# One indirect transfer of 128 rows per expert pair, replaced by two of 64 rows, in a decoder layer with 64 experts

## The reference

```python
x = _layernorm(x + attention(x))
x = _layernorm(x + cross_attention(x, ctx))
x = _layernorm(x + _moe(x))                      # E = 64, K = 8, H = 256, I = 96, CAP = 64

def _moe(hidden_states, gate_w, wg, wu, wd):
    x = hidden_states.reshape(-1, Hd)            # T = 1024 tokens
    probs = jax.nn.softmax(x @ gate_w.T, axis=-1)
    w, sel = jax.lax.top_k(probs, K)
    w = w / jnp.sum(w, axis=-1, keepdims=True)
    eid, tok = sel.reshape(-1), jnp.repeat(jnp.arange(T), K)
    ...
    valid = pos < CAP                            # an expert takes its first 64 tokens
    xin = jnp.zeros((E, CAP + 1, Hd), x.dtype).at[eid, slot].set(x[tok])
    h = silu(einsum("ech,ehi->eci", inp, wg)) * einsum("ech,ehi->eci", inp, wu)
    out = einsum("eci,eih->ech", h, wd)
    y = jnp.zeros((T, Hd), x.dtype).at[tok].add(out_pad[eid, slot] * w * valid)
```

## Time and profile before

| | |
|---|---|
| median of 3 runs | 375.88 us (374.93 to 377.12) |
| the profiled execution | 371.15 us, of which the span from first to last instruction is 369.2 us |
| mean granted TensorE clock | 0.845 of full speed |
| PE busy | 266.0 us (72% of the span) |
| DVE busy | 232.5 us (63%) |
| POOL busy | 164.0 us (44%), of it 49.7 us in the 32 scatters of L599 |
| ACT busy | 131.8 us (36%) |
| DMA | 66.61 MB, mean 180 GB/s |

### The profile page before, as it was taken

The page is one execution under the profiler, slowest core; times in us unless marked ns, Lnnn a source line. Parts: engine busy times, 40 slices in busy tenths (PEclk is TensorE's granted clock), DMA queues, the critical chain, the costliest instruction groups (busy, mean ns, idle before and its releaser), DMA issues.

```text
span 369.2 us, 5446 instructions
## 1 busy us (share of the span) xinstructions
PE 266.0 (72%) x1793; PEld 167.1 (45%) x1793; DVE 232.5 (63%) x532; ACT 131.8 (36%) x234; POOL 164.0 (44%) x167
## 2 busy tenths in 40 slices
PE   8676696899889897898888787105899999980000
PEld 4462464567466574575455554002344554540000
DVE  0927754499876999678944777503335777750692
ACT  4510375017941169511494134000123444440021
POOL 2002022400253446825545077876144588874272
PEclk9695899899999999999989699655557999995555
DMA  7799908789999221961110299971999898655981
GB/s 251 226 123 276 311 10 119 110 241 301 385 323 194 80 93 71 164 125 71 66 63 3 65 333 317 288 219 34 267 285 304 211 159 144 75 64 101 364 324 57
DMA packets 47261, 66.61 MB, mean 180 GB/s; under 512 B 5979, under 2 KB 33241, under 8 KB 47234
## 3 DMA queue, kind: packets, MB, share of 16 engines
q1 hardware_dynamic: 39120, 56.52, 55.4%
q0 software_dynamic: 7680, 9.47, 13.7%
q10 hardware_dynamic: 434, 0.27, 0.2%
HBM read 36.45 MB, written 28.75 MB: 177 GB/s over the span
## 4 chain that ended last, share of the span: by engine, by line
PE 38%; DVE 27%; issue 9%; DMA 9%; ACT 8%; SPq 4%; POOL 3%; POOLq 0%; DVEq 0%; ACTq 0%
PE M L1314 14%; PE SA L1314 6%; DVE nmax L908 6%; PE O L1314 5%; PE SB L1314 5%; DMA early<-early 4%; SPq L379 4%; PE O L1787 3%; POOL xin_d L517 3%; ACT probs L640 2%; DVE early L1274 2%; DVE early L1280 2%; DVE xmax L899 1%; PE SB L1807 1%; DMA early<-acc_d 1%
## 5 line engine op out<-in xcount | busy, mean ns | idle before, releaser
L599 POOL DMA_INDIRECT acc_d<-xp_t,idx_out x32 | 49.7, 1552 | 30.1 <-ACT xp_t L821 19.1
L504 POOL DMA_INDIRECT xin_d<-row,idx_slot x48 | 47.7, 994 | 34.1 <-DVE nmax L908 12.0
L1314 PE MATMUL M<-middle 128*128 128x256 f32 (+3 forms) x144 | 29.0, 385 | 3.9 <-ACT middle L676 1.2
L1314 PE MATMUL SA<-early 96*128 96x256 bf16 (+1 forms) x128 | 22.4, 305 | 8.5 <-DMA early<-early 3.5
L808 ACT ACTIVATE xp<-M 128x96 f32<-128x96 f32 x32 | 8.0, 250 | 56.1 <-PE M L1314 56.1
L558 POOL TENSOR_TENSOR early<-early 128x1024 f32<-128x1024 f32 x3 | 6.4, 2140 | 46.5 <-ACT early L650 46.4
L1314 PEld LDWEIGHTS M<-middle 128*128 128x128 f32 (+1 forms) x144 | 20.6, 197 | 11.8 <-issue 6.2
L908 DVE TENSOR_REDUCE nmax<-SA 128x4 f32<-128x1024 f32 x16 | 19.5, 1218 | 9.1 <-PE SA L1314 9.1
L1787 PE MATMUL O<-con,probs 128*128 128x128 f32 x40 | 10.3, 345 | 19.6 <-DMA probs<-xin_d 19.6
L1314 PE MATMUL SB<-early 96*128 96x256 bf16 (+1 forms) x128 | 21.5, 296 | 3.5 <-DVE nmax L908 2.4
L1314 PE MATMUL O<-middle,early 128*128 128x256 f32 (+1 forms) x96 | 20.9, 364 | 2.7 <-DVE middle L948 2.5
(11 more groups left out here) (261 smaller groups left out, 623.9 us busy)
## 6 DMA issues: line engine op xcount, KB each, us to landing
acc_d<-zeros SPq DMA_DIRECT2D x3, 2176.0 KB, 17.1
early<-early SPq DMA_DIRECT2D x48, 128.0 KB, 5.1
early<-acc_d SPq DMA_DIRECT2D x24, 256.0 KB, 5.8
xin_d<-zeros SPq DMA_DIRECT2D x1, 5136.0 KB, 20.1
early<-wgu SPq DMA_DIRECT2D x12, 384.0 KB, 13.3
middle<-wgu SPq DMA_DIRECT2D x12, 384.0 KB, 7.7
probs<-xin_d SPq DMA_DIRECT2D x20, 160.5 KB, 2.7
gu_sb<-wgu SPq DMA_DIRECT2D x8, 384.0 KB, 6.4
```

Of the source, the lines that this page charges most:

```text
L504: nc.gpsimd.indirect_dma_start(xin_d, bass.IndirectOffsetOnAxis(ap=idx[:, t, k:k + 1], axis=0), rows[:, t, :], None, bounds_check=SLOTS - ...
L599: nc.gpsimd.indirect_dma_start(acc_d[p % CHAINS], bass.IndirectOffsetOnAxis(ap=idx_out[:, p:p + 1], axis=0), yw[:, p % YRING, :], None, bo ...
L1314: return nc.tensor.matmul(o, l, r, start=start, stop=stop)
```

## The change

Each pair's rows leave in two transfers of 64 rows, one for each expert. There are four chains: pair p's expert e goes to chain 2 x (p mod 2) + e, so that a chain is used again two pairs later. Inside one transfer each token occurs once, so a chain needs one row per token: keys are no longer doubled, nothing is added for the second expert, and the index tile `idx_out` gets a column for each half, both on partitions 0 to 63 (DVE writes them with two instructions in place of one). A chain has 1152 rows in place of 2176. At the end SP reads two tiles of one chain with one load, 16 loads in all. It waits for chains 0 and 1 first and issues four loads from them, then waits for chains 2 and 3. DVE adds 2 x 256 columns to 2 x 256, and one more sum of 256 closes the tile.

```diff
-ROWS = NTOK + CAP
+ROWS = NTOK + P
-CHAINS = 3
+CHAINS = 4
...
-        idx_out = sb("idx_out", [P, PAIRS], I32)
+        idx_out = sb("idx_out", [P, 2, PAIRS], I32)
...
-        acc_d = [nc.dram_tensor(f"acc_d{c}", [2 * ROWS, D], F32, kind="Internal").ap() for c in range(CHAINS)]
+        acc_d = [nc.dram_tensor(f"acc_d{c}", [ROWS, D], F32, kind="Internal").ap() for c in range(CHAINS)]
...
-            for c in range(CHAINS):
-                sp.wait_ge(S["scat"][c], 16 * len(range(c, PAIRS, CHAINS)))
-            for t in range(TILES):
-                for c in range(CHAINS):
-                    sp.dma_start(fin[:, t, 2 * c:2 * c + 2, :],
-                                 acc_d[c].rearrange("(r h) d -> r h d", h=2)[t * P:(t + 1) * P]).then_inc(S["gu"][t], 16)
+            def load_sums(u, chains):
+                for c in chains:
+                    sp.dma_start(fin[:, 2 * u:2 * u + 2, c, :],
+                                 acc_d[c][2 * u * P:2 * (u + 1) * P].rearrange("(t p) d -> p t d", t=2)
+                                 ).then_inc(S["gu"][2 * u], 16)
+
+            for c in range(2):
+                sp.wait_ge(S["scat"][c], 16 * (PAIRS // 2))
+            for u in range(2):
+                load_sums(u, range(2))
+            for c in range(2, CHAINS):
+                sp.wait_ge(S["scat"][c], 16 * (PAIRS // 2))
+            for u in range(2):
+                load_sums(u, range(2, CHAINS))
+            for u in range(2, TILES // 2):
+                load_sums(u, range(CHAINS))
...
+                pool.wait_ge(S["idx_out"], 2 * (p + 1))
                 pool.wait_ge(S["yw"], p + 1)
-                if p >= CHAINS:
-
-                    pool.wait_ge(S["scat"][p % CHAINS], 16 * (p // CHAINS))
-                nc.gpsimd.indirect_dma_start(acc_d[p % CHAINS], bass.IndirectOffsetOnAxis(ap=idx_out[:, p:p + 1], axis=0),
-                                             yw[:, p % YRING, :], None, bounds_check=2 * ROWS - 1, oob_is_err=True,
-                                             compute_op=ALU.add).then_inc(S["scat"][p % CHAINS], 16)
+                for e in range(2):
+                    c = 2 * (p % 2) + e
+                    h = slice(e * CAP, (e + 1) * CAP)
+                    if p >= 2:
+
+                        pool.wait_ge(S["scat"][c], 16 * (p // 2))
+                    nc.gpsimd.indirect_dma_start(acc_d[c], bass.IndirectOffsetOnAxis(ap=idx_out[0:CAP, e, p:p + 1], axis=0),
+                                                 yw[h, p % YRING, :], None, bounds_check=ROWS - 1, oob_is_err=True,
+                                                 compute_op=ALU.add).then_inc(S["scat"][c], 16)
...
-                        act.wait_ge(S["scat"][(p - YRING) % CHAINS], 16 * ((p - YRING) // CHAINS + 1))
+                        for e in range(2):
+                            act.wait_ge(S["scat"][2 * ((p - YRING) % 2) + e], 16 * ((p - YRING) // 2 + 1))
...
-                    nc.vector.tensor_scalar(idx_out[:, p:p + 1], gath(p)[:, D + E:ROW], half, None, ALU.add
-                                            ).then_inc(S["idx_out"], 1)
+                    for e in range(2):
+                        nc.vector.tensor_scalar(idx_out[0:CAP, e, p:p + 1], gath(p)[e * CAP:(e + 1) * CAP, D + E:ROW], 0.0, None,
+                                                ALU.add).then_inc(S["idx_out"], 1)
...
-                dve.wait_ge(S["gu"][t], fin_base[t] + 16 * CHAINS)
-                nc.vector.tensor_tensor(fin[:, t, 0:3], fin[:, t, 0:3], fin[:, t, 3:6], ALU.add).then_inc(S["fpair"], 1)
-
-            def thirds_added(t, c):
+                u = t - t % 2
+                dve.wait_ge(S["gu"][u], fin_base[u] + 16 * CHAINS)
+                nc.vector.tensor_tensor(fin[:, t, 0:2], fin[:, t, 0:2], fin[:, t, 2:4], ALU.add).then_inc(S["fpair"], 1)
+
+            def quarters_added(t):
                 dve.wait_ge(S["fpair"], t + 1)
-                if c == 2:
-                    dve.wait_ge(S["fadd"], 2 * t + 1)
-                nc.vector.tensor_tensor(fin[:, t, 0], fin[:, t, 0], fin[:, t, c], ALU.add).then_inc(S["fadd"], 1)
+                nc.vector.tensor_tensor(fin[:, t, 0], fin[:, t, 0], fin[:, t, 1], ALU.add).then_inc(S["fadd"], 1)
...
-                    thirds_added(i, 1)
...
-                    thirds_added(i, 2)
+                    quarters_added(i)
...
-    con[:, CONST["key"]] = 2 * (np.arange(NT) * P + p)
-    con[:, CONST["dump"]] = 2 * (NTOK + p % CAP)
+    con[:, CONST["key"]] = np.arange(NT) * P + p
+    con[:, CONST["dump"]] = NTOK + p % CAP
```

More of the change, by code:

```diff
@@ L232, in loaded @@
             return S["gu"][n % RING], 32 * (n // RING + 1)
-        ACCS = 2 * CHAINS
+        ACCS = CHAINS
         fin = early[:, 0:TILES * ACCS * D].rearrange("p (t f d) -> p t f d", t=TILES, f=ACCS)
@@ L294, in build @@
             S[n] = ctx.enter_context(nc.semaphore(n))
-        S["gu"] = [ctx.enter_context(nc.semaphore(f"gu_in{r}")) for r in range(max(RING, TILES))]
+        S["gu"] = [ctx.enter_context(nc.semaphore(f"gu_in{r}")) for r in range(max(RING, TILES - 1))]
         S["gath"] = [ctx.enter_context(nc.semaphore(f"gathered{r}")) for r in range(GRING)]
@@ L369, in iteration @@
                         sp.dma_start(acc_d[n].rearrange("(p r) d -> p r d", p=P),
-                                     zeros[:, 0:D].unsqueeze(1).broadcast_to([P, 2 * ROWS // P, D])
+                                     zeros[:, 0:D].unsqueeze(1).broadcast_to([P, ROWS // P, D])
                                      ).then_inc(S["zero_out"], 16)
@@ L394, in rows_out @@
                 sp.wait_ge(S["zero_out"], 16 * (1 + CHAINS))
-                sp.dma_start(acc_d[0][0:2 * NTOK].rearrange("(b t p h) d -> b h p t d", t=NT, p=P, h=2)[b, 0],
+                sp.dma_start(acc_d[0][0:NTOK].rearrange("(b t p) d -> b p t d", t=NT, p=P)[b],
                              rows[:, :, 0:D]).then_inc(S["row_out"], 16)
@@ L430, in _ @@
                     sp.wait_ge(S["hid"], 2 * (p + 1))
-                    sp.wait_ge(S["idx_out"], p + 1)
+                    sp.wait_ge(S["idx_out"], 2 * (p + 1))
                     load_rows(p + GRING)
@@ L593, in scatter @@
             def scatter(p):
-                pool.wait_ge(S["idx_out"], p + 1)
+                pool.wait_ge(S["idx_out"], 2 * (p + 1))
                 pool.wait_ge(S["yw"], p + 1)
-                if p >= CHAINS:
-                    pool.wait_ge(S["scat"][p % CHAINS], 16 * (p // CHAINS))
-                nc.gpsimd.indirect_dma_start(acc_d[p % CHAINS], bass.IndirectOffsetOnAxis(ap=idx_out[:, p:p + 1], axis=0),
-                                             yw[:, p % YRING, :], None, bounds_check=2 * ROWS - 1, oob_is_err=True,
-                                             compute_op=ALU.add).then_inc(S["scat"][p % CHAINS], 16)
+                for e in range(2):
[6 more added lines that the diff above has]
+                                                 compute_op=ALU.add).then_inc(S["scat"][c], 16)
             for p in range(PAIRS):
@@ L1036, in route @@
                     need(dve, "keycol", b, 1)
-                    nc.vector.tensor_scalar(keycol[:], keycol[:], 2.0 * T, None, ALU.add).then_inc(S["keycol"], 1)
+                    nc.vector.tensor_scalar(keycol[:], keycol[:], float(T), None, ALU.add).then_inc(S["keycol"], 1)
                 def slots():
@@ L1243, in _ @@
             pipelined(iteration, last_batch)
-            half = con[:, CONST["half_of_row"]][:, 1:2]
             for i in range(PAIRS + 1):
@@ L1272, in halves_added @@
             def halves_added(t):
-                dve.wait_ge(S["gu"][t], fin_base[t] + 16 * CHAINS)
-                nc.vector.tensor_tensor(fin[:, t, 0:3], fin[:, t, 0:3], fin[:, t, 3:6], ALU.add).then_inc(S["fpair"], 1)
-            def thirds_added(t, c):
+                u = t - t % 2
+                dve.wait_ge(S["gu"][u], fin_base[u] + 16 * CHAINS)
+                nc.vector.tensor_tensor(fin[:, t, 0:2], fin[:, t, 0:2], fin[:, t, 2:4], ALU.add).then_inc(S["fpair"], 1)
+            def quarters_added(t):
                 dve.wait_ge(S["fpair"], t + 1)
-                if c == 2:
-                    dve.wait_ge(S["fadd"], 2 * t + 1)
-                nc.vector.tensor_tensor(fin[:, t, 0], fin[:, t, 0], fin[:, t, c], ALU.add).then_inc(S["fadd"], 1)
+                nc.vector.tensor_tensor(fin[:, t, 0], fin[:, t, 0], fin[:, t, 1], ALU.add).then_inc(S["fadd"], 1)
             def row_stats(t):
-                dve.wait_ge(S["fadd"], 2 * t + 2)
+                dve.wait_ge(S["fadd"], t + 1)
                 nc.vector.bn_stats(fstats[:, t], fin[:, t, 0]).then_inc(S["fstat"], 1)
```

## The result

The changed kernel takes 413.82 us (median of 4 runs, 411.76 to 417.42), the kernel before on the same chip 375.4 us (4 runs): 1.107 times as long, 95% interval 1.094 to 1.121. The forecast was 386.3 us, with a range up to 402. It was slower, as forecast, but by 38 us in place of 10.

What follows compares the result with a forecast made beforehand. POOL was taken to set when sums may be read and, with 2.54 us per pair against PE's 2.00, to become the bound: last landing +16.0, end -5.6, so +10.4 on 375.88 gives 386.3 us, range 374 to 402.

Steps and rivals of the forecast that it cites:

- X: POOL's price for one 64-row accumulating scatter, estimated at 0.97 us between bounds of 0.78 and 1.55.
- 54 X: POOL's issue of two 64-row scatters for each of 27 pairs, 5 to 31, in the total 54 X - 43.5 + w.
- The upper bound of 1.55: Ceiling set on X: a 64-row scatter costs at most a whole 128-row one, 1.55 us.
- rival 3: On POOL, a scatter's price doesn't fall at all with half the rows, X = 1.55: 417 us; chance 0.06.
- rivals 2 and 3: Scatter price on POOL: 2, plain price fixed, X = 1.26, 400.9 us, chance 0.22; 3, price unchanged, 417 us, 0.06.
- w: POOL's waits for earlier scatters of a chain to land, on top of issue: 1.5 us taken, 0 to 4.2 possible.
- rival 1: On POOL, scatter generation is all per row, X = 0.78, with w about 3: 377.3 us; chance 0.17.
- Pairs 0 to 4 in the slow part: Half-clock stretch, scatters 3.53 us apart: 2.54 us per pair on POOL fits, so pair 5 starts at 282.76 as before.
- The end: Loads and closing sums after the last landing: 1.3 us saved to the first sum, 4.3 over eight tiles, 5.6 together.
- Terms held at nothing: DVE's extra index instruction, ACT's wait for both halves, PE's pace or clock drop, smaller zeroing: nothing at the end.
- Rivals 1 and 4: Scatter price on POOL: 1, all per row, 377.3 us, chance 0.17; 4, accumulating surcharge a stall, 367 us, 0.10.
- The 43.5: Constant subtracted in the forecast difference from the kernel before, 54 X - 43.5 + w, in us.

Runs made afterwards that it cites:

- the price table: Kernel before plus 84 indirect transfers of 14 kinds after its last store; accumulating 64 rows took 1.42 us on POOL; its total time says nothing.

## Why the prediction was wrong

**The price of a 64-row scatter: the step that failed.** I took X = 0.97 us, on the assumption that 0.58 us of the plain price and all of the 0.58 us for accumulating are work per row. Measured: 1.40 us, of which 1.25 are there with no rows. Per row it is 2.4 ns, a quarter of what I had assumed (1.16 us for 128 rows is 9 ns per row). The term 54 X is 75.8 us in place of 52.4: +23.4. This alone puts the forecast at 409.7. Each of the two numbers that I had, 0.97 plain and 1.55 accumulating at the same 128 rows, says nothing on how a price depends on rows; I treated their difference as if it did. The upper bound of 1.55 was the nearer one, and what was said against rival 3 ("accumulating more rows must cost something") was right by 0.15 us only. The truth lay between rivals 2 and 3, to which I gave 0.28 together, with a range that ended below rival 3.

The Trainium skill's figure of about 1 us for the software path's emission (DMA: Bandwidth & Descriptors, "Latency and other measured facts") pointed the right way: plain transfers have 0.84 us that rows don't change, accumulating ones 1.25. The Trainium skill's rule not to split a transfer over partition halves (DMA: Bandwidth & Descriptors, "Rules for kernel authors") held as well: 1.107 times the time. The reason that the Trainium skill gives there is that the two serialize on the DMA engines; what shows in this kernel is the second instruction on POOL.

**The waits on landings, w.** Taken 1.5 us, bounds 0 to 4.2; measured 3.7 (111.5 against 107.86 with three pairs between). Inside the bounds, but for another reason than mine. I compared the distances between two uses of a chain in the fast part (5.08 and 5.55 us) and left out the 0.8 us from a landing to the next start. The waits fell earlier, in pairs 2 and 4: in the slow part two pairs are 7.0 us apart where three were 10.6, and the first scatter took 7.9 us to land.

```profile
287.69 1.40 POOL L612 DMA_INDIRECT acc_d<-xp_t,idx_out  x1 [1.49 <-DVE idx_out L1264]
289.70 1.40 POOL L612 DMA_INDIRECT acc_d<-xp_t,idx_out  x1 [0.61 <-issue]
291.85 1.40 POOL L612 DMA_INDIRECT acc_d<-xp_t,idx_out  x1 [0.75 <-DMA acc_d<-xp_t,idx_out]
```

(The first of these rows names DVE, whose indices for this pair had been written by 281 us; the pair's chain was last used at 279.69, so this too is a landing.) With a cheap X such waits matter much more, as the runs with half the scatters show (11 us); rival 1's 377 us was too low for that reason as well.

**Pairs 0 to 4 in the slow part.** I let pair 5 start as before, 17.6 us after the first scatter, since 2.54 is below 3.53. It started 20.9 us after it (291.85 against 270.94), 3.3 us late: nearly all of w stands here, in a stretch that I had left without waits, and from pair 5 on POOL waited hardly at all. The instructions alone don't do it: with 3.41 us per pair against 3.53, pair 5 starts 17.4 us after the first where chains come back after three pairs. POOL is the bound from the first scatter, and the clock's rise brings nothing.

**The end.** Forecast 5.6 us saved after the last landing. To ACT's last instruction it saved 5.8, but 2.6 of this are lost again behind that instruction, so 3.2 us remain (30.4 to 27.2), within the bounds of 2.3 to 7.6. The landing itself came 1.05 us later after its start. In the run with four sums alone, from the last scatter's start, 5.5 us are saved. First sum after the landing: 3.9 forecast, 3.4 measured; pace per tile 1.6 forecast, 1.55 measured (394.72 to 404.04 for six tiles). What was not foreseen is the stall of 1.5 us before the third tile's first sum, the slower landing and the 2.6 us at the very end. POOL's L621 takes 0.69 us beside the narrower sum and 0.23 without one, as L608 did.

**Terms held at nothing.** DVE's second index instruction, ACT's wait and PE's pace cost nothing at the end, since POOL hid them. PE's granted clock was 1.00 from 282 to 328 us, with PE busy 2.1 to 3.0 of every 4 us from 304 on; it was 0.50 from there to 334, 1.00 again from 337 to 349, and 0.50 from 352 on. That too was hidden. The zeroing goes from 6.7 to 4.7 MB, not from 6.5 to 4.6, which changes nothing.

**The sum with measured terms.** 54 x 1.403 - 43.5 + 3.7 = +36.0. The 43.5 holds 5.6 us for the end and 2.23 from the last instruction's end to its landing, which measured 3.2 and 3.43: 3.6 us more, +39.6 against 39.5 from the first scatter's start to the end of the span, and 38.4 in the medians. The mechanism was right; its main term was 23 us too small. Rivals 1 and 4, with X = 0.78 and 0.49, are excluded by the price table: even 16 accumulating rows cost 1.29.

## What to carry to other kernels

Ask of an instruction what it costs with almost no rows before splitting it: two durations at one size give no slope, and a small test of four sizes does. Where an engine issues back to back, as POOL here with 0.15 us of slack per pair, an added instruction of any size is paid almost in full. The time before an accumulator can be used again is landing plus hand-over, 3.8 + 0.8 us here; divide it by the number of pairs between two uses and compare it with the pace of the engine that feeds them, and not only with POOL's own price. Where landings are slow, as behind full DMA engines (7.9 us here), two pairs between uses can be too few even for a slow feeder.

## What was not expected of the hardware

- An accumulating indirect transfer holds POOL for 1.29 us with 16 rows and 1.56 with 128; a plain one for 0.86 and 0.99. Neither row length (128, 256 or 321 floats) nor traffic beside changed the median by more than 0.03 us; single instructions took up to 0.08 more.
- 0.8 us pass from a scatter's landing to the start of the next one in its chain, 0.30 us between two instructions that wait for nothing.
- With four loads of 256 KB issued beside it, the last scatter's landing took 4.8 us in place of 3.1 (3.7 in the run with first halves only, where they were issued 1.2 us after its start); with eight, 5.3 in place of 3.8. Each is one execution.
